# One block of ScalarE work moved within its slot: a fused Mamba + mixture-of-experts kernel

## The reference, cut to what matters

```python
h = _layernorm(x) * (1 + ca) + sa
x = x + ga * attn(h)            # norm, then a Mamba scan forwards and one backwards
h = _layernorm(x) * (1 + cb) + sb
x = x + gb * ffn(h)             # 8 experts, top 2 by gate, and one shared expert

# scan, over 16 states for each of 256 inner channels:
h = exp(dt_t * A) * h + (dt_t * u_t) * B_t ;  y_t = sum_n h * C_t
# an expert:
h = x @ w1 ;  h * sigmoid(h) * (x @ w2) @ w3
```

## Time and profile before

| | |
|---|---|
| median of 3 runs | 2608.18 us |
| the profiled execution, as timed | 2608.1 us |
| its span in the profile | 2606.3 us |
| VectorE busy | 2288.7 us, 88% |
| TensorE matmul busy | 2115.5 us, 81% |
| GpSimd busy | 1957.9 us, 75% |
| ScalarE busy | 1510.3 us, 58% |
| DMA engines | 33% of the span, 113 GB/s |

### The profile page before, as it was taken

How to read it: one execution, slowest core, us unless ns; L and a number is a source line. 1 busy time by engine, 2 the same in 40 slices (tenths; PEclk the granted TensorE clock), 3 DMA queues, 4 the chain that set the end, 5 groups by cost and what they waited for, 6 DMA issues and landing times. The chain is left out here.

```text
span 2606.3 us, 37957 instructions
## 1 busy us (share of the span) xinstructions
PE 2115.5 (81%) x9893; PEld 1352.7 (52%) x9893; DVE 2288.7 (88%) x3603; ACT 1510.3 (58%) x2468; POOL 1957.9 (75%) x1437
## 2 busy tenths in 40 slices
PE   3677887878788797888879788797978879798868
PEld 1244554545555455555546555454555545555554
DVE  1699998989899898998989899899989989899973
ACT  2546656655565665656666555665556566565633
POOL 1577878778787877878777787877878787787854
PEclk8777998989899898998989899898989989899989
DMA  2334233333323333332333323233332333333310
GB/s 82 129 130 138 102 131 106 110 127 113 130 98 128 108 114 122 113 125 103 114 124 115 135 97 130 106 109 127 113 130 97 128 108 114 122 113 124 114 67 5
DMA packets 120494, 293.33 MB, mean 113 GB/s; under 512 B 18516, under 2 KB 53172, under 8 KB 120388
## 3 DMA queue, kind: packets, MB, share of 16 engines
q1 hardware_dynamic: 120388, 292.30, 32.8%
HBM read 285.91 MB, written 6.34 MB: 112 GB/s over the span
## 5 line engine op out<-in xcount | busy, mean ns | idle before, releaser
L426 POOL TENSOR_TENSOR bt<-v,bb 128x1024 f32<-128x1024 f32 x512 | 1207.1, 2361 | 176.5 <-DVE psA L787 173.7
L787 DVE TENSOR_TENSOR_SCAN psA<-psA,bt 128x512 f32<-128x512 f32 x1024 | 1199.4, 1218 | 114.4 <-POOL bt L426 91.6
L600 ACT ACTIVATE psA<-dt,aneg 128x512 f32<-128x512 f32 x1024 | 688.1, 688 | 821.0 <-DVE g L797 816.3
L987 PEld LDWEIGHTS psY<-ident,g 128*128 128x128 f32 x4096 | 519.4, 152 | 474.7 <-DVE g L797 262.3
L987 PE MATMUL psY<-ident,g 128*128 128x128 f32 x4096 | 608.6, 295 | 160.9 <-DVE g L797 160.7
L797 DVE TENSOR_TENSOR g<-psA,cb 128x512 f32<-128x512 f32 x1024 | 676.0, 680 | 0.0
L526 POOL TENSOR_TENSOR act<-pf,gf 128x512 f32<-128x512 f32 x288 | 366.2, 1272 | 252.1 <-DVE pf L882 220.9
L1068 PE MATMUL F<-h2T,w 128*128 128x512 f32 x576 | 334.2, 664 | 92.9 <-DVE pf L882 92.9
L1112 PE MATMUL F<-w,act 128*128 128x128 f32 x2304 | 318.6, 283 | 43.7 <-POOL act L526 41.7
L1112 PEld LDWEIGHTS F<-w,act 128*128 128x128 f32 x2304 | 291.4, 198 | 60.9 <-issue 53.9
L1071 PE MATMUL F<-h2T,w 128*128 128x512 f32 x576 | 308.9, 619 | 0.0
(11 more groups left out here) (133 smaller groups left out, 1724.6 us busy)
## 6 DMA issues: line engine op xcount, KB each, us to landing
bb<-bc_rows SPq DMA_DIRECT2D x256, 512.0 KB, 3.6
cb<-bc_rows SPq DMA_DIRECT2D x256, 512.0 KB, 3.6
x<-in_L_attn_x SPq DMA_DIRECT2D x16, 256.0 KB, 3.8
xR<-in_L_attn_x SPq DMA_DIRECT2D x16, 256.0 KB, 3.6
out_x<-osb SPq DMA_DIRECT2D x16, 256.0 KB, 3.9
w<-in_L_ffn_ew SPq DMA_DIRECT2D x2, 1024.0 KB
modA<-mod_table SPq DMA_DIRECT2D x16, 128.0 KB, 3.9
bc_rows<-xd SPq DMA_DIRECT2D x32, 64.0 KB, 3.0
```

The lines of the kernel that those rows point to most:

```text
L426: g.tensor_tensor(bt[:, n % 2, :, :], v[d][:, :, :], bb[:, n // 2 % 2, n % 2, :].unsqueeze(1).broadcast_to([P, NH, T]), ALU.mult).then_inc ...
L600: s.activation(psA[:, half * T:half * T + T], dt_[d][:, half, :], ACT.Exp, scale=aneg[d][:, half, n:n + 1]).then_inc(a_s, 1)
L787: w.tensor_tensor_scan(ah, ah, bt[:, n % 2, half, :][:, order], 0.0, ALU.mult, ALU.add)\
L987: last = m.matmul(psY[:, half * T + i * P:half * T + i * P + P], g_[:, n % 2, half, i * P:i * P + P], ident[:, :], is_transpose=True, star ...
```

## The change

The two instructions of an expert turn leave `expert_turns`, which ran first in the slot after the products, and stand now in ScalarE's `ffn_side`, in the slot in which the products are made. Against `before`, the stream of ScalarE differs only in where a turn stands: it moves ahead of the side work of its own slot (and of the `facc` copy of slot 13 and of `keep_y` of slot 16). Instructions, their sizes and their waits stay as they are, and so do the streams of all other engines.

```diff
-            def expert_turns(fb, k):
-
-                if k is not None:
-                    at = 2 * NE * fb + k
-                    act_e.wait_ge(F0_full, at + 1)
-                    wait(act_e, pf_s, at - 1)
-                    s.activation(tf[:, k % 2, :], F0[:, :], ACT.Tanh, scale=0.5).then_inc(tf_s, 1)
-                    act_e.wait_ge(F1_full, at + 1)
-                    wait(act_e, act_s, at - 2)
-                    s.activation(gf[:, k % 3, :], F1[:, :], ACT.Copy).then_inc(F1_free, 1)
-
             def ffn_side(fb, slot):
...
                 if slot == GATE_SLOT + 2:
                     act_e.wait_ge(gate_s, GATES * fb + GATE_D)
                     s.activation(ge[:, :], gd[:, :], ACT.Exp).then_inc(ge_s, 1)
+                k = up_at(slot)
+                if k is not None:
+                    at = 2 * NE * fb + k
+                    act_e.wait_ge(F0_full, at + 1)
+                    wait(act_e, pf_s, at - 1)
+                    s.activation(tf[:, k % 2, :], F0[:, :], ACT.Tanh, scale=0.5).then_inc(tf_s, 1)
+                    act_e.wait_ge(F1_full, at + 1)
+                    wait(act_e, act_s, at - 2)
+                    s.activation(gf[:, k % 3, :], F1[:, :], ACT.Copy).then_inc(F1_free, 1)
                 if down_at(slot) == (0, 1):
                     act_e.wait_ge(F2_full, (DOWN + NE) * fb + DOWN + 1)
                     wait(act_e, o_s, 2 * fb)
...
                     if slot == N and scan:
                         keep_y(b, 0)
-                    if ffn:
-                        expert_turns(b - 1, up_at(slot - 1))
                     if scan and nxt < STEPS:
```

## The result

The changed kernel takes 2625.28 us, the median of 4 runs (2624.6 to 2626.51), against 2608.28 us before. The ratio is 1.0061, with a 95% interval of 1.0048 to 1.0076 (ratios are taken over the single runs, so they can differ a little from the quotient of two medians). That is 17 us or 0.6% slower, 13 us more than forecast and outside the forecast range. The profiled execution of after is one of 2627.43 us with a span of 2625.6 us, which is 19.3 us longer than the span before; what follows is read against those 19.3 us.

What follows compares the result with a forecast made beforehand. VectorE, 88% busy, was taken as busiest, with ScalarE's order deciding in slots with side work. Sum: 2608.1 - 2.0 (slot 9) + 4.9 (slots 26 to 28) + 1.3 (tail) = 2612.3, said as 2612 us, range 2604 to 2618.

Steps and rivals of the forecast that it cites:

- the first of slot 9: Slot 9, ScalarE: the table reload stays in place, tf takes th's place at 1342.32, and pf comes 0.49 us earlier.
- -2.0 us for slot 10 in 15 passes: Turn ahead of th in slot 9: five passes each at -0.49, -0.29 and +0.37 us, summing to -2.0 us.
- the forecast's +4.2: Whole kernel: -2.0 for slot 9, +4.9 for slots 26 to 28 and +1.3 for the tail, against the profiled execution.
- the worst that slot 9 was given: Upper bound of the slot 9 term, +5.5 us, if F1 of turn 0 ended late in all 15 passes.
- low-clock stretches that move: Sign of being wrong above all: a pass whose timeline matches and whose length does not; no size given.
- the first sign of its list: Slot 10, VectorE: the gap before pf falls from 2.02 to 1.53 us in all passes.
- The three kinds of slot 9: Passes by length of the F1 product (1.02, 1.33 or 1.92 us): -0.49, -0.29 or +0.37 us, five passes each.
- Slots 26 to 28: Turn ahead of dt: slot 29's scan 0.57 us late, 0.35 surviving in each of passes 1 to 14, +4.9 us.
- The rival in which the stall carries in full: Slot 29: if th does not hold zs, 14 x 0.57 = +8.0 us instead of 4.9, 2615.4 us; chance 0.15.
- The covers elsewhere: Slots 10, 11, 13, 15, 16, 20, 23, 25: side work up to 2.2 us later still in time, costed at nothing.
- The tail: Slot 13's facc copy stands behind the turn, and TensorE, which needs that buffer, waits: +1.3 us, once.
- The slow stretch falls on F1 in every pass: Rival: F1 of turn 0 late in all passes, slot 9 costs +5.5 us, total 2619.8 us; chance 0.12 (most passes).

Runs made afterwards that it cites:

- e1: The changed kernel with a one-column tanh, which has no wait, put ahead of the turn in slot 9: 2612.76 us against 2609.81 for the kernel before, ratio 1.0017.
- e9: The changed kernel with the two waits ahead of tf swapped, pf_s first and F0_full last: 2614.21 us against 2610.4 for the kernel before, ratio 1.0017.

## Why the prediction was wrong, step by step

*The step that failed* is the first of slot 9: "The table reload ahead of the first tanh stays where it is, so `tf` takes the place of `th` at 1342.32". It holds in pass 1 and pass 15 and fails in the 13 loop passes, where the load follows the wait for F0. The load starts 1.24 us later than in before (3.67 us after the first scan of slot 10 instead of 2.43), `tf` ahead of `th` gives 0.49 of it back, and 0.75 is left, which is the +0.74 measured. The forecast took the place of the load from the trace of before, in which the activation behind it had a single wait. It did not ask how the program issues an activation that has two. e1 and e9 are the proof. The forecast's -2.0 us for slot 10 in 15 passes came out at +9.9 - 0.34 = +9.6, so this step is 11.6 of the 15.1 us between the forecast's +4.2 and the 19.3 of the profiled span. The price of the failure did not lie in any bound either: +5.5 was the worst that slot 9 was given. Nor was it the sign that the forecast had named for being wrong, low-clock stretches that move; it stood in the first sign of its list, the gap before `pf`, which went from 2.02 to 2.77 us in the loop passes and not to 1.53.

The Trainium skill ("ScalarE: Activation LUTs", Step-by-step: what each stage is for) says that where the table isn't active the compiler has placed a table load right before the activation. The trace agrees: the 1.28 us load stands directly ahead of `tf`. The cost hangs on what the sentence leaves open, whether the load comes before or behind the activation's waits.

*The three kinds of slot 9* were right as mechanism and size, wherever the load stood free: -0.49, between, and +0.35 in e9, against -0.49, -0.29 and +0.37 forecast. Pass 1 of after shows the slow kind (+0.34). In after's loop passes they were hidden, since `gf` comes 1.9 us after the end of F0 by then and never waits for F1. How many passes fall to each kind could not be read from before: e9 has seven quick and two slow ones among its 13 loop passes, where five of each kind among 15 had been carried over.

*Slots 26 to 28* were right. Counted from F1 of slot 26, the exponentials for slot 29 start 7.16 us later in before and 8.09 in after, 0.93 later where 0.92 was forecast; TensorE's `dt` product and the F1 behind it moved by 0.14 us where 0.12 was forecast. The gap before the scan is 0.72 us (forecast about 0.8), the wait for `th` 1.36 (about 1.4), and 0.34 us a pass survives, +4.8 us in all for +4.9. By slots it is -0.23 in slot 27, +0.81 in slot 28 and -0.24 in slot 29; the first two make 0.58 us of lateness, where 0.57 was forecast. The rival in which the stall carries in full is excluded by slot 29, which gives 0.24 us back.

*The covers elsewhere* held: in passes 1 to 14 no other slot but slot 1 changed its mean by more than 0.05 us. Slot 25 gave pass 15 a gain of 0.99 us that was not foreseen. The order did not make it: that slot has a granted clock of 0.72 and takes 6.05 us in before, and has 1.00 and takes 5.06 in after. Over all thirteen kernels, with turn 15 moved or not, it takes 5.06 us in the six in which no low clock falls on it and 6.02 to 6.07 in the seven in which it does.

*The tail* has the forecast wait, 1.27 us for 1.3, and pays 1.5 us for it. It grew by 3.0 us, though. The other 1.4 us come before its first turn, at TensorE's two products (L1024 and L1026 in before, L1020 and L1022 in after) that end the scan part. From the start of the first to the end of the second, before and after (length, then busy times, then the granted clock):

```profile
2524.62:2526.64 2.02, 2.02 (x10) 1.35 (x10) 0.00 (x0) 0.00 (x0) 1.50 (x2) 1.00 0.00 0
2540.72:2544.41 3.69, 3.68 (x10) 2.42 (x10) 0.00 (x0) 0.00 (x0) 1.75 (x2) 0.54 0.06 15
```

The same work at the low clock costs 1.67 us more here, of which 1.4 reach VectorE.

*Slot 1* adds 1.4 us in the same way. The thirteen kernels have 195 slots 1 in passes 1 to 15. In 108 of them the low clock covers at most 0.03 us, and they take 4.04 us. In 87 it covers over 2 us; 81 of these take 4.23 to 4.71 us and six 5.42. Its sum over passes 1 to 14 shifts by -1.9 to +1.7 us from kernel to kernel without the order in it being touched. The start and pass 0, +1.0 us, hold no turn at all; before the first scan the thirteen kernels take 87.1 to 90.4 us. So 9.6 + 4.8 + 1.5 = 15.9 of the 19.3 us are the change's own, and 3.4 lie where no moved turn was found to act, most of them with the clock or the start. Why the stretches at the low clock moved was not tried and stays open.

*The rivals.* None had this mechanism. "The slow stretch falls on F1 in every pass" came nearest in time, 2619.8 us, and has nothing to do with it: F1 was of all three kinds.

## What to carry to other kernels

Before moving an activation across a table switch, find the load that the builder will put in front of it and list the waits of that activation: a load hides beside a wait only if it is issued before it. With several waits, put ahead the one that is met long before, and look at the written-out passes separately from the loop's, as the same source can give opposite orders. If two instructions of a unit wait for different things, here F0 and F1, move only the one whose input is there: `tf` alone gained 6.8 us over 14 passes. The pair, with the load out of the wait, gained 3.4 in e9, with a loss in the passes whose F1 was late.

## What was unexpected

- A table load without work to hide it cost 0.74 us a pass, less than its 1.28 us: it came 1.24 us later, and the early `tf` gave 0.49 back at the same time.
- The Trainium skill ("ScalarE: Activation LUTs", What ACT_TABLE_LOAD costs) gives about 1283 ns for the load and about 1380 ns more of drain, 2.66 us for a switch. The rows show the load, 1.28 us, and no drain: in after the logarithm starts at 1038.25, the load before it at 1036.96, 1.29 us from start to start, and in e9's loop pass it is 1.30. For this kernel the measured 1.3 us decides.
- Two moves that are harmless or cheap alone cost more together: -3.1 us for turn 16, +2.6 for turn 17, +4.75 for both, because the 0.23 us a pass that turn 16 gains in slot 27 are lost in the stall behind it, and because it delays TensorE's product by 0.14 us, for which turn 17 makes ScalarE wait. 14 x (0.23 + 0.14) = 5.2 us is the difference between +4.75 and -3.1 + 2.6.
- Places whose order the change did not touch still differ by a few us between two traces of one execution each. A stretch is to be compared at the same granted clock before its difference is put down to the change.
